# A graph network kernel: slot reductions in two edge loops replaced by halving trees of adds

## The reference

```python
# layer 0: attention without a softmax over neighbours; H = 4 heads, D = 16
score = jnp.exp(jnp.clip(jnp.sum(k[src] * q[dst], axis=-1) / SCALE, -5.0, 5.0))
wv = jax.ops.segment_sum(v[src] * score[..., None], dst, num_segments=n)
z = jax.ops.segment_sum(score, dst, num_segments=n)
...
# layer 1: sum, sum of squares, min and max of an edge vector h of 64 channels
h = jnp.concatenate([xi, xj, ea], axis=-1) @ Wpre + bpre
s1 = jax.ops.segment_sum(h, dst, num_segments=n_nodes)
s2 = jax.ops.segment_sum(h * h, dst, num_segments=n_nodes)
mn = jnp.where(has, jax.ops.segment_min(h, dst, num_segments=n_nodes), 0.0)
mx = jnp.where(has, jax.ops.segment_max(h, dst, num_segments=n_nodes), 0.0)
```

## Time and profile before

| what | value |
|---|---|
| median of 3 runs | 3039.01 us (3038.76 to 3039.15) |
| profiled execution | 3039.15 us, span 3037.5 us |
| busy over the span | VectorE 69%, GpSimd 59%, TensorE 48%, ScalarE 39% |
| loop 0, gathers of GpSimd | about 171 to 1317 us |
| loop 1, gathers of GpSimd | about 1425 to 2497 us |
| granted TensorE clock | 0.60 of full speed, mean |

### The profile page before, as it was taken

How to read it: one execution, slowest core, us unless ns; L and a number is a source line. 1 busy time by engine, 2 the same in 40 slices (tenths; PEclk the granted TensorE clock), 3 DMA queues, 4 the chain that set the end, 5 groups by cost and what they waited for, 6 DMA issues and landing times.

```text
span 3037.5 us, 28803 instructions
## 1 busy us (share of the span) xinstructions
PE 1456.8 (48%) x4543; PEld 634.3 (21%) x4544; DVE 2098.9 (69%) x3559; ACT 1191.9 (39%) x3184; POOL 1791.5 (59%) x1818
## 2 busy tenths in 40 slices
PE   2125555656545443344444444443443233497975
PEld 2101111212111111122111111111111003474542
DVE  6847777878756666675778888886677786513176
ACT  0013334434334334430556666665555553010121
POOL 3457777777777777721777777677777760000213
PEclk7556666666666566665555555555555556598965
DMA  5232222222222222210222222222221110173200
GB/s 137 52 75 58 57 62 58 59 57 57 56 61 61 58 61 63 66 27 23 57 57 58 68 58 59 61 59 57 57 58 43 30 27 2 54 270 130 88 1 11
DMA packets 124334, 186.48 MB, mean 61 GB/s; under 512 B 62045, under 2 KB 79154, under 8 KB 124127
## 3 DMA queue, kind: packets, MB, share of 16 engines
q0 software_dynamic: 57776, 89.59, 14.6%
q1 hardware_dynamic: 48894, 70.70, 7.2%
q10 hardware_dynamic: 17618, 25.71, 2.4%
HBM read 146.04 MB, written 39.84 MB: 61 GB/s over the span
## 4 chain that ended last, share of the span: by engine, by line
POOL 15%; PE 14%; issue 11%; DVE 9%; ACT 6%; DVEq 2%; DMA 2%; POOLq 2%; ACTq 0%; SPq 0%
POOL arena L544 15%; PE mm L683 4%; ACT arena L1049 3%; PE l L878 3%; DVE red L1661 3%; PE mm L817 2%; PE l L904 1%; PE tp L667 1%; PE mm L878 1%; PE hist L878 1%; PE mm L904 1%; DMA arena<-kv_tab,rec 1%; POOLq L630 1%; POOLq L624 1%; DVE arena L1684 1%
## 5 line engine op out<-in xcount | busy, mean ns | idle before, releaser
L544 POOL DMA_INDIRECT arena<-b_tab,lin x815 | 809.8, 994 | 371.5 <-issue 247.5
L544 POOL DMA_INDIRECT arena<-kv_tab,rec x815 | 811.0, 995 | 258.7 <-issue 232.0
L737 PE MATMUL l<-arena,identB 128*128 128x512 bf16 x996 | 394.8, 564 | 527.9 <-DVE arena L1544 518.7
L1049 ACT ACTIVATE arena<-arena,lin 128x64 f32<-128x64 f32 x1984 | 479.6, 333 | 0.0
L1661 DVE TENSOR_REDUCE red<-arena 128x128 f32<-128x2048 f32 x189 | 459.6, 2486 | 13.6 <-issue 12.8
L817 PE MATMUL mm<-Wslots,eaT 48*128 48x512 f32 x248 | 234.2, 1097 | 399.5 <-ACT eaT L1043 390.1
L1544 DVE TENSOR_SCALAR arena<-arena,digit 128x512 bf16<-128x512 int16 x744 | 257.4, 415 | 57.1 <-PE l L737 43.1
L759 PE MATMUL hist<-arena,oh_lo 125*128 125x225 bf16 x400 | 170.7, 584 | 244.9 <-DVE arena L1515 244.9
L737 PEld LDWEIGHTS l<-arena,identB 128*128 128x128 bf16 x996 | 116.0, 128 | 799.1 <-DVE arena L1544 620.0
L544 POOL DMA_INDIRECT arena<-cnt_tab,infoR x25 | 26.7, 1069 | 374.3 <-DVEq L1832 366.9
L1046 ACT ACTIVATE arena<-arena 128x1024 f32<-128x1024 f32 x62 | 65.6, 1057 | 447.5 <-DVE arena L1684 447.5
(11 more groups left out here) (381 smaller groups left out, 2444.6 us busy)
## 6 DMA issues: line engine op xcount, KB each, us to landing
arena<-at_tab SPq DMA_DIRECT2D x50, 800.0 KB, 5.9
at_tab<-T ACTq DMA_DIRECT2D x25, 800.0 KB, 3.4
arena<-kv_tab,rec POOLq DMA_INDIRECT x815, 2.6
arena<-b_tab,lin POOLq DMA_INDIRECT x815
at_pack<-arena SPq DMA_DIRECT2D x25, 256.0 KB
T<-at_pack SPq DMA_DIRECT2D x25, 256.0 KB, 2.7
lin_tab<-lin ACTq DMA_DIRECT2D x62, 64.0 KB, 1.6
lin<-lin_tab SPq DMA_DIRECT2D x62, 56.0 KB
```

What stands on the lines that cost most here:

```text
L544: return pool.indirect_dma_start(dst, None, table, offs(ap=index, axis=0))
L737: last = pe.matmul(l3[:, 0, :], identB[:], hot[:, j], start=False, stop=True, skip_group_check=True)
L1049: last = act.activation(dst[:, s], hh[u][:, s, 0:C], ACT.Identity, bias=bias[:, s:s + 1])
```

## The change

The reduction over the 16 slots is written as levels of adds (or maxima, minima) in place: 8 rows take in the other 8, then 4, 2 and 1. In loop 1 that is twelve two-input instructions with a drain after each level instead of three reductions with one drain. In loop 0 there are three levels (8, 4, 2), and the last two rows are added to the accumulator one after the other. The scratch tile `red` becomes smaller.

```diff
-        red = sb("red", [P, 4 * C])
+        red = sb("red", [P, 2 * C + 4])
...
-                red_(red[:, 0:C + HEADS], weighted[u].rearrange("p s c -> p c s"), X_AXIS, ALU.add)
-                d()
-                v_ = accV[:, bass.ds(blk, 1), :]
-                tt(v_, v_, red[:, 0:C + HEADS].unsqueeze(1), ALU.add)
-                d()
+                for n in (8, 4, 2):
+                    tt(weighted[u][:, 0:n], weighted[u][:, 0:n], weighted[u][:, n:2 * n], ALU.add)
+                    d()
+                for k in range(2):
+                    v_ = accV[:, bass.ds(blk, 1), :]
+                    tt(v_, v_, weighted[u][:, k:k + 1], ALU.add)
+                    d()
...
-                parts = ((hh[u], accS, ALU.add, red[:, 0:2 * C]), (hmax[u], accMx, ALU.max, red[:, 2 * C:3 * C]),
-                         (hmin[u], accMn, ALU.min, red[:, 3 * C:4 * C]))
+                folds = ((hh[u], accS, ALU.add), (hmax[u], accMx, ALU.max), (hmin[u], accMn, ALU.min))
                 dve.wait_ge(hmin_ready, g + 1)
-                for t, acc, op, r in parts:
-                    red_(r, t.rearrange("p s c -> p c s"), X_AXIS, op)
-                d()
-                for t, acc, op, r in parts:
+                for n in (8, 4, 2, 1):
+                    for t, acc, op in folds:
+                        tt(t[:, 0:n], t[:, 0:n], t[:, n:2 * n], op)
+                    d()
+                for t, acc, op in folds:
                     v_ = acc[:, bass.ds(blk, 1), :]
-                    tt(v_, v_, r.unsqueeze(1), op)
+                    tt(v_, v_, t[:, 0:1], op)
                 d()
```

## The result

The changed kernel takes 3085.46 us (median of 4, 3084.12 to 3089.38) where the kernel before took 3038.89 us in runs beside it: ratio 1.0156, 95% interval 1.0139 to 1.0174. It is 1.6% slower; the forecast was 3084. The profiled execution has a span of 3080.5 us against 3037.5.

A forecast was written before the change was run, and what follows sets the result against it. GpSimd was taken to bound both loops in about two thirds of their steps. Loop 1's gathers and waits +45, its end -4 and loop 0 +4 us gave 3084 us, range 3058 to 3103.

The forecast's parts named there:

- GpSimd bounds both loops: Loops 0 and 1: GpSimd sets the pace in about two thirds of steps and has almost no slack otherwise.
- the 14.9 us of waits: Loop 1: GpSimd's time waiting for others, the most that VectorE's shorter step could win back.
- VectorE's levels: Loop 1 on VectorE: four levels take about 5.5 us a step in place of 7.30 us of reductions.
- one moment: Each gather, 0.13 us after its start, needs something that an instruction with both inputs in SBUF holds until its end.
- 1.12 us a step: Loop 1 on GpSimd: stretch of gathers by the levels per step, from a schedule summing to 1.1 to 1.25 us.
- +66 us less 6: Loop 1 on GpSimd: 59 steps of added gather stretch, +66 us, against some 6 us of present stretches that go.
- The 11 odd steps: Loop 1: steps with the first moment at 1.33 us, expected to become like the 48 at 0.26 to 0.37.
- End of loop 1, -4: After loop 1's last gather: VectorE takes up the last rows sooner and the last block is 1.8 us shorter, together -4 us.
- Loop 0, +4 (0 to 12): Loop 0: VectorE gains nothing; the 272-element add stretches a gather by 0.12 us in some 42 steps, +4 us.
- (a): Rival, loop 1: short adds let gathers through, so the levels cost GpSimd nothing; 3020 us, chance 0.07.
- (b): Rival, loop 1: moments spread evenly over the 1.25 us between gathers, 0.69 us a step; 3063 us, chance 0.08.
- (c): Rival: 1.25 us a step in loop 1, present stretches unchanged, loop 0 at 8; 3105 us, chance 0.05.

The follow-up runs named there:

- the PSUM operand: Changed kernel with the second operand of each loop 1 level read from PSUM, slots not reduced: 3031.26 us, ratio 0.9969.
- the one-input reductions: Changed kernel with loop 1's twelve adds, minima and maxima replaced by reductions over a length-one axis, slots not reduced: 3024.61 us, one run.
- the two shifted kernels: Changed kernel with an unused reduction ahead of loop 1's levels, starting them 0.40 us later (3037.69 us) or 0.13 us later (3066.45 us).
- the first experiments: Early follow-up runs, not listed one by one; the first two told have levels in loop 1 alone (3087.07 us) or loop 0 alone (3044.12 us).

## Why the prediction was right, point by point

- *GpSimd bounds both loops, and VectorE's saving is worth at most the 14.9 us of waits.* Right: VectorE lost 158 us of work, and its wait for rows grew from 135.7 to 309.4 (forecast 290). The 14.9 us of GpSimd's waits went.
- *VectorE's levels.* 5.5 us forecast, 5.41 measured; 512 elements 0.69 and 0.688, 256 elements 0.425 and 0.421. The 2293 ns that the prediction quotes beside this sum stand in the `tensor_tensor` row of the tier table in the Trainium skill's "VectorE: DVE Perf Modes"; for `tensor_reduce` that table gives the 1x mode and no time. The sum doesn't use them.
- *A gather has one moment 0.13 us after its start, and an instruction with two SBUF inputs holds it from 0.16 us after that instruction's start until its end.* Shown by the PSUM operand and by the one-input reductions (same count and sizes, no stretch beside them, 54 and 61 us less), by the two shifted kernels, and by the edge of the hold between 0.14 and 0.19 us. The rule is too narrow for VectorE as a whole, since L1690, with one tensor from SBUF, holds as well; the change adds no such instruction.
- *1.12 us a step, +66 us less 6.* All stretches of loop 1 went from 41.0 to 101.2, +60.2, as forecast, but by two errors that cancel: the levels cost 62.7 us and not 66 (most steps have 1.0 to 1.13 us), and the other stretches fell by 2.4 and not by 6. Less the 14.9 us of waits this is +45; the loop grew by 48.7, since the gaps under "issue" grew by 3.2 us (247.5 to 250.7), a term that the sum doesn't have. Last gather forecast at 2546, measured at 2545.3. The 11 odd steps did what was said of them: after the change 5 steps have their first moment elsewhere than 0.26 to 0.37 us.
- *End of loop 1, -4.* Measured -4.8 from the last gather to the end of the span: VectorE takes up the last rows 2.0 us sooner, and the last block is 1.7 us shorter (5.41 against 7.13). The saving of the next-to-last block is hidden, as forecast: the last one now waits 2.69 us for ScalarE in place of 0.88.
- *Loop 0, +4 (0 to 12).* The levels stretch gathers by 6.4 us, but L1521 now stretches them by 6.8 in place of 9.7, and GpSimd's wait for its buffer fell from 7.3 to 2.9: the loop is 0.2 us longer in the profile (1145.1 against 1144.9). Over all traces, the six with levels in loop 0 give 1146.2 us for it on average, the three with the reduction and the tile as before 1144.3. With loop 0 alone changed the runs give +4.9 (2.1 to 7.6 by the interval). So the term is right in sign, and its size is open between some 2 and 5 us.
- *The rivals.* (a), short adds let gathers through, is excluded by the stretches that the 512-element and smaller adds cause: 8.5 us by the 256-element adds alone, and 12.6 us by the 512-element adds in the kernel with the levels 0.13 us later. Here the Trainium skill, "SBUF — State Buffer", § Who interferes with whom, is borne out in its rule for instructions with two SBUF inputs; its inference that `tensor_tensor` leaves descriptor generation alone does not carry over to gathers whose index tile lies in SBUF. That the index read is the moment is argued from that section, and no run moved the index elsewhere. (b), spread moments, did not come about: 56 of 61 first moments stand at 0.26 to 0.37 us after the change. Its price was a little low: by the prediction's own schedule (holds from 0.16 us after an add's start, drains of 0.12) an even spread gives 0.77 us a step and not 0.69, which is 3068 and not 3063. Of (c), 1.25 us a step was above every step measured, though one of its parts, that present stretches hardly fall, came true.
- The closeness of 3084 to 3085.46 is partly luck. In the profiled executions +45 - 4 + 4 became +48.7 - 4.8 + 0.2, with 1.1 us less ahead of and between the loops, +43.0 in all: errors of some 4 us that cancel. And single runs of the changed kernel lie from 3082.18 to 3089.38, and 24 runs of the kernel before, beside the first experiments, from 3033.44 to 3045.13. The trace's own sums (60.2 and 62.7 us of stretch, the last gather) are the firmer evidence.

## What to carry to other kernels

Ask of a rewrite on VectorE not only how long it takes but what it holds while it runs: if GpSimd issues gathers on the critical path, an add with two SBUF inputs costs GpSimd what is left of it at the gather's moment, and a reduction or an add with one operand in PSUM cost nothing here. Read the offset between the two engines in the timeline, since a regular loop repeats it in every step; 0.4 us of added work moved it and gave 48 us back. Where a reduction is slow, look at the order in which it reads before replacing it, and let an engine that holds nothing do the strided writing, if its writes are small: ScalarE's writes of 64 elements bore it, its square of 1024 didn't.

## What the runs showed of the hardware that I had not expected

- The hold lets a gather in at the border between two adds that follow each other without a drain: each was stretched to the end of the one add it met, never through the next.
- In the product that writes at a stride the hold ends before the instruction: the gather of 961.50 ends at 963.29, 0.71 us after the product (962.58) and not 0.81. So it is with all 61 gathers that meet it (0.69 to 0.72).
- A strided access cost VectorE about as much in writing as in reading: 1.940 us for 1024 elements written at a stride of 64 B against 1.226 (one operand of that product, the repeated scores, lies at the same stride there, and no run separates the two), and 1.88 for 1024 elements read at a stride of 256 B against 1.20 side by side. ScalarE's large square behaves alike (1.97 against 1.06), its small writes of 64 elements (0.388 against 0.333) hardly.
